# A graph layer and a routed feed-forward layer on one core: sorting nodes by expert during the gather stage, and edge steps of two octets

## The reference

```python
msgs = features[edge_src] * edge_weight[:, None]          # features = layernorm(x)
agg  = segment_sum(msgs, edge_dst, num_segments=12500)
x    = x + einsum('ni,oi->no', agg, W) + b
xf   = layernorm(x)
H    = gelu(xf @ W1 + b1, approximate=False)              # 1024 hidden columns
probs = softmax(H @ Wg + bg)                              # 8 experts
assign = argmax(probs)
out  = x + probs[:, assign] * (H @ Wd[assign] + bd[assign])   # Wd: 8 x 1024 x 256
```

## Time and profile before

| | us |
|---|---|
| median of 3 runs | 3659.71 (3659.63 to 3661.93) |
| the profiled execution | 3686.61 |
| its span, first to last instruction | 3684.6 |
| gather stage (105.38 to 3088.04) | 2982.66 |
| last group, routing, 105 routed tiles | 596.6 |

### The profile page before, as it was taken

One profiled execution on the slowest core, in us unless ns is written; L12 is line 12 of the kernel. 1 busy time (PEld: TensorE's weight loads), 2 busy tenths in 40 slices (PEclk: granted clock), 3 DMA queues, 4 the chain that ended last, 5 costly groups with the idle time before them and its releaser, 6 DMA issues.

```text
span 3684.6 us, 40719 instructions
## 1 busy us (share of the span) xinstructions
PE 2061.4 (56%) x10526; PEld 1319.5 (36%) x10527; DVE 1151.1 (31%) x3507; ACT 443.2 (12%) x847; POOL 1822.5 (49%) x1988
## 2 busy tenths in 40 slices
PE   0134555455535554455445544555355548599998
PEld 0112332233323332233223322332233324488887
DVE  8121332233323332233223322332133224733332
ACT  5000000000000000000000000000000002043343
POOL 1656445644565445544664455444644540055554
PEclk9995666566656666566656656666566658799999
DMA  8323332333333332333233323332333231455554
GB/s 358 88 82 98 97 103 84 115 99 98 104 91 106 100 101 83 113 100 101 84 115 100 102 81 111 98 102 86 105 103 100 82 92 63 154 180 180 181 184 139
DMA packets 153598, 420.31 MB, mean 114 GB/s; under 512 B 33320, under 2 KB 67499, under 8 KB 150880
## 3 DMA queue, kind: packets, MB, share of 16 engines
q0 software_dynamic: 100032, 300.27, 27.6%
q1 hardware_dynamic: 53536, 119.73, 8.8%
HBM read 328.02 MB, written 92.82 MB: 114 GB/s over the span
## 4 chain that ended last, share of the span: by engine, by line
PE 38%; another core or an unknown queue 33%; issue 15%; DVE 7%; DVEq 5%; ACT 1%; DMA 0%; POOL 0%; ACTq 0%; POOLq 0%
PE psH L557 8%; PE psE L507 6%; PE psA L638 3%; PE psG L638 2%; PE psH L638 2%; PE psE L638 2%; PE psA L578 2%; PE psG L499 2%; PE psR L499 2%; PE psA L535 2%; DVEq L301 2%; DVE rows L942 1%; DVEq L295 1%; PE psG L564 1%
## 5 line engine op out<-in xcount | busy, mean ns | idle before, releaser
L387 POOL DMA_INDIRECT big<-xn_table,src_i x1664 | 1590.8, 956 | 1427.4 <-PE psG L499 620.8
L507 PE MATMUL psE<-place,parts 128*128 128x64 f32 x1664 | 450.8, 433 | 1015.3 <-DVE parts L853 778.4
L507 PEld LDWEIGHTS psE<-place,parts 128*128 128x128 f32 x1664 | 382.6, 324 | 1280.6 <-DVE parts L853 871.7
L557 PE MATMUL psH<-xn2T,w 128*128 128x512 f32 x800 | 427.9, 692 | 128.6 <-issue 64.5
L450 ACT ACTIVATE hidT<-psH,b 128x512 f32<-128x512 f32 x200 | 136.4, 687 | 2447.2 <-remote 1006.6
L499 PE MATMUL psR<-big,sel_narrow 128*32 128x256 f32 x1664 | 216.8, 613 | 289.4 <-issue 289.4
L557 PEld LDWEIGHTS psH<-xn2T,w 128*128 128x128 f32 x800 | 173.4, 223 | 347.8 <-issue 267.6
L860 DVE TENSOR_TENSOR big<-psE,big 128x128 f32 x416 | 121.2, 291 | 545.1 <-remote 294.3
L853 DVE COPY parts<-psR 128x256 f32<-128x256 f32 x208 | 88.0, 423 | 518.6 <-remote 461.2
L499 PE MATMUL psG<-big,sel_narrow 128*32 128x256 f32 x1664 | 217.6, 613 | 0.0
L864 DVE TENSOR_TENSOR place<-iota,shift_f 128x256 f32<-128x256 f32 x104 | 44.4, 427 | 447.7 <-issue 447.7
(11 more groups left out here) (194 smaller groups left out, 2193.4 us busy)
## 6 DMA issues: line engine op xcount, KB each, us to landing
row_table<-rows SPq DMA_DIRECT2D x25, 2064.0 KB
big<-xn_table,src_i POOLq DMA_INDIRECT x1664
big<-in_x SPq DMA_DIRECT2D x10, 1280.0 KB, 17.5
xn_table<-big SPq DMA_DIRECT2D x10, 1280.0 KB, 12.9
big<-in_x SPq DMA_DIRECT2D x25, 512.0 KB
row_table<-big SPq DMA_DIRECT2D x25, 512.0 KB, 3.0
big<-in_Wd SPq DMA_DIRECT2D x8, 1024.0 KB, 12.0
hidT<-in_dstT SPq DMA_DIRECT2D x2, 840.0 KB, 30.3
```

The costliest lines, as they stand in the source:

```text
L387: nc.gpsimd.indirect_dma_start(out=xring[:, h * STEP_TILES + j, :], out_offset=None, in_=xn_dram[:, :], in_offset=bass.IndirectOffsetOnAxi ...
L507: mm = nc.tensor.matmul(psE[q % 2][:, k * NARROW:(k + 1) * NARROW], parts[:, q % 2, k * P:(k + 1) * P], place[:, q, :], start=True, stop=True)
L557: mm = nc.tensor.matmul(psH[c % 2][:, :], w1[:, k, c * P:(c + 1) * P], xn2T[:, k, :], start=(k == 0), stop=(k == KC - 1))
```

## The change

**Edge steps.** A section is now two octets of eight tiles. Pairs of tiles share 32 lanes (16 each) and accumulate in PSUM, so 16 partial matmuls (still 256 columns each) fill one `psQ` of 512 columns; DVE copies it once; four place matmuls of 80 columns replace eight of 64; two adds replace four; one table operation each replaces two. `s_edge_mm` rises once, by 16, after all 16 partials, instead of by 4 after each quad. The wide way, for sections whose tiles or octets span too many nodes, stays.

```diff
-                    def partial(q):
-
-                        pe.wait_ge(s_narrow, g * 2 + q // 2 + 1)
-                        for j in range(QUAD):
-                            t = h * STEP_TILES + q * QUAD + j
-                            mm = nc.tensor.matmul(psQ[q % 2][j * LANES:(j + 1) * LANES, 0:C], sel_narrow[:, t, :],
-                                                  xring[:, t, :], start=True, stop=True)
-                        mm.then_inc(s_edge_mm, QUAD)
...
+                    pe.wait_ge(s_narrow, g + 1)
+                    for o in range(OCTS):
+                        for odd in range(2):
+                            for j in range(OCT // 2):
+                                t = h * STEP_TILES + o * OCT + 2 * j + odd
+                                mm = nc.tensor.matmul(psQ[j * LANES:(j + 1) * LANES, o * C:(o + 1) * C],
+                                                      sel_narrow[:, t, :], xring[:, t, :],
+                                                      start=(odd == 0), stop=(odd == 1))
+                    mm.then_inc(s_edge_mm, STEP_TILES)
+
+                    pe.wait_ge(s_parts, g + 1)
+                    for o in range(OCTS):
+                        for k in range(KC):
+                            at = (o * KC + k) * SPAN
+                            mm = nc.tensor.matmul(psE[:, at:at + SPAN], parts[:, o, k * P:(k + 1) * P],
+                                                  place[:, o, :], start=True, stop=True)
+                    mm.then_inc(s_placed, 1)
```

```diff
+            def routed_hidden(r, i):
+
+                pe.wait_ge(s_c2, r + 2)
+                for c in range(HC):
+                    if c % 4 == 0:
+                        pe.wait_ge(s_g2, r * HC + c + 4)
+                    for k in range(KC):
+                        mm = nc.tensor.matmul(psH[c // 4][:, (c % 4) * P:(c % 4 + 1) * P],
+                                              w1[:, k, c * P:(c + 1) * P], xT2[i][:, k * P:(k + 1) * P],
+                                              start=(k == 0), stop=(k == KC - 1))
+                    if c % 4 == 3:
+                        mm.then_inc(s_h2, 1)
+
+            def product(r, i, rounds):
+
+                pe.wait_ge(s_wl[i], rounds * 16 + 16)
+                pe.wait_ge(s_r2, r + 1)
+                for c in range(HC):
+                    pe.wait_ge(s_g2, r * HC + c + 1 + HC)
+                    mm = nc.tensor.matmul(psY[:, 0:C], hT2[:, c, :], wd[:, i, c, :],
+                                          start=(c == 0), stop=(c == HC - 1))
+                mm.then_inc(s_y2, 1)
```

```diff
-                with pe.If(kind == SECTIONS):
-                    before = n.with_bounds(min_val=0, max_val=NF - 2)
-                    hidden(before, before + 1)
-                    transpose_xn2(before + 1)
+                with pe.If(kind == SECTIONS):
+                    part_a(n.with_bounds(min_val=0, max_val=LAST - 1), QB)
+                with pe.If(kind == SECTIONS + 1):
+                    part_b(n.with_bounds(min_val=0, max_val=LAST - 1), QB)
```

More of the change, by code:

```diff
@@ L190, in build @@
[L190 to L196, removed]
@@ L271, in build @@
+        s_i2 = sem("routed_ids_dve")
         s_o2 = sem("routed_out_ready")
[L272 to L295, removed]
@@ L297, in step_field @@
-        def step_field(load, k, a, b, engine, top):
-            return load(steps_i[0:1, bass.ds(k, 1), a:b].rearrange("a b c -> a (b c)"), engine, top)
+        s_os = [sem(f"routed_out_stored{i}") for i in range(RING2)]
+        s_back = [sem(f"routed_out_loaded{h}") for h in range(SECTIONS)]
+        s_out = [sem(f"out_scattered{h}") for h in range(SECTIONS)]
         def load_columns(ap, engine, top):
@@ L303, in load_columns, with step_field, step_count, tiles_of @@
                 skip_runtime_bounds_check_because="columns and kinds are worked out within their bounds")[1]
+        def step_field(k, a, b, engine, top):
+            return load_columns(steps_i[0:1, bass.ds(k, 1), a:b].rearrange("a b c -> a (b c)"), engine, top)
+        def step_count(k, a, eng, engine):
+            raw, = nc.values_load_multi_w_load_instructions(
+                steps_i[0:1, bass.ds(k, 1), a:a + 1].rearrange("a b c -> a (b c)"), engines=(engine,),
+                skip_runtime_bounds_check_because="cut to its low eight bits below")[1]
+            return eng.snap(raw & 255, min_val=0, max_val=255).with_bounds(min_val=0, max_val=NG)
+        def tiles_of(f):
+            return [f * PER_GROUP + i for i in range(PER_GROUP)]
         block = ctx.enter_context(nc.Block())
@@ L368, in _ @@
+            for a in range(0, REST, PER_GROUP):
+                for j, (row, expert) in enumerate(tile_plan(a, min(a + PER_GROUP, REST))):
+                    load_tile(EARLY + a + j, row, expert)
         @block.gpsimd
@@ L381, in _ @@
             pool.wait_ge(s_xn_stored, 16 * LN_CHUNKS)
-            def gather_section(g):
+            for g in range(NG):
                 h = g % SECTIONS
@@ L431, in _ @@
+            for j in range(REST):
+                pool.wait_ge(s_o2, EARLY + j + 1)
+                scatter(late_rows[:, j, :], EARLY + j, s_out[0])
+            totals = [16 * sum(len(batches[b]) for b in range(h, len(batches), SECTIONS)) for h in range(SECTIONS)]
+            totals[0] += 16 * REST
+            for h in range(SECTIONS):
+                pool.wait_ge(s_out[h], totals[h])
         @block.scalar
@@ L447, in hidden @@
[L447 removed]
+                    nc.scalar.activation(xn2T[:, k, 0:nq * P], psH[k][:, 0:nq * P], ACT.Identity).then_inc(s_xtc, 1)
                 for c in range(HC):
                     act.wait_ge(s_h, f * HC + c + 1)
[L450 removed]
+                    nc.scalar.activation(hidT[:, c, 0:nq * P], psH[c % 2][:, 0:nq * P], ACT.Gelu,
                                          bias=b1[:, c:c + 1]).then_inc(s_gelu, 1)
@@ L478, in _ @@
+            copy_routed(EARLY)
+            for r in range(EARLY, NR):
+                gelu_routed(r)
+                if r + 1 < NR:
+                    copy_routed(r + 1)
+                residual(r)
         @block.tensor
@@ L586, in hidden, with gate @@
-                mm.then_inc(s_g, 1)
+                def gate():
+                    pe.wait_ge(s_gc, f + 1)
+                    pe.wait_ge(s_c2, f * PER_GROUP + 2 + 2)
+                    for q in range(nq):
+                        mm = nc.tensor.matmul(psL[:, q, :], gate_parts[:, q * P:(q + 1) * P],
+                                              fold[:, :], start=True, stop=True)
+                    mm.then_inc(s_g, 1)
+                routed_pair(f * PER_GROUP + 2, f * 2 + 1, gate, lambda: pe.wait_ge(s_dif, f + 1))
@@ L655, in _ @@
+            part_a(LAST, LAST_QB)
+            part_b(LAST, LAST_QB)
+            pe.wait_ge(s_ev, LAST * QB + LAST_QB + 1)
+            transposes(EARLY, 0, EARLY // RING2)
+            for r in range(EARLY, NR):
+                routed_hidden(r, r % RING2)
+                if r + 1 < NR:
+                    transposes(r + 1, (r + 1) % RING2, (r + 1) // RING2)
+                product(r, r % RING2, r // RING2)
         @block.vector
@@ L1104 @@
+            for r in range(EARLY, NR):
+                routed_out(r, r % RING2, r - EARLY, r // RING2, True)
 def kernel(**inputs):
```

1130 lines of the change are left out of this document (613 added, 517 removed).

## The result

The changed kernel takes 4275.25 us (median of 4 runs, 4268.27 to 4314.99), the kernel before 3659.67: ratio 1.171, 95% interval 1.165 to 1.177. It is slower by 616 us. The forecast was 4155. The profiled execution is the 4315 one (span 4313.3); the forecast's sum for a profiled execution was 4181, so 132 us are missing from it.

The account below looks back on a forecast made before the run. PE's chain with DVE, its results told late while POOL issues gathers, bounds the gather stage. Start 115, stage 3845 and end 221 make 4181; plus 2, less 27 gives about 4155 us, range 3250 to 4480.

Parts of the forecast that it names:

- the stall: Gather stage: PE's matmuls are told as done late while POOL issues gathers; 979 us before, 9.4 a section.
- The sum at full speed: Whole changed kernel without late PE results: 115 start, 967 gather steps, 1872 groups, 221 end, together 3175 us.
- The stall in the changed kernel: Gather stage after the change: PE's results still come late beside POOL's issuing, 9.7 us a section, stage 3845 us.
- 6.5 us for each part: Parts A and B of each group: each follows a step and loses 6.5 us to late PE results.
- a gather step, table reading and branch about 3.2 us: Gather step: table reading and branch take about 3.2 us of the 9.3 us forecast for the step.
- 48 steps come right after a part and run at 9.3: Gather stage: 48 steps after a part, with POOL's ring full, run at 9.3 us each, 446 us together.
- Both waits are met at once, so POOL issues 20 us without a break: POOL's gathers: both section waits are met after all 16 partials, so 16 gathers at 1.25 us go out unbroken.
- The end: After the last gather step: last group's parts, plan and block copies, 16 late tiles; 221 us instead of 597.
- SP is late: Rival: SP's ordered store, copies and loads delay each part's tiles 10 us, 480 more; chance 0.14 shared with a longer stall.
- Two routed tiles in each part, the hidden layer twice: Groups: two routed tiles a part, 14.2 us, hidden layer computed twice; parts 27 and 51, 1054 us more in all.
- no stall: Rival: the number of hand-overs in edge steps, not POOL's issuing, slows PE; steps run at 9.3, 3150 us; chance 0.14.
- half a stall: Rival: with fewer hand-overs a stalled gather step costs perhaps 3.5 us, giving 3514 us; chance 0.18.

Follow-up runs that it names:

- a_nowide: The changed kernel with the never-taken wide way's code and its branch removed from PE and DVE, gathers as they are: 4295 us.
- a_nowide_nogather: The changed kernel without the wide way's code on PE and DVE, and with only the first 48 gathers issued: 3085 us.
- a_nw_memset: The changed kernel without the wide way's code, each gather after the first 48 replaced by four POOL memsets on an unread tile: 3080 us.
- b_nogather: The kernel before with only the first 48 gathers issued, their rows read again for every section: 2702 us.
- a_nw_pause4: The changed kernel without the wide way's code, POOL waiting after every fourth gather until its gathers land: 3552 us, 0.971 of the kernel before.

## Why the prediction was right, and where it was not

The direction and the size held: 4155 forecast, 4275 measured, inside 3250 to 4480. The way to it did not quite: the changed kernel is braked mostly by something that the forecast did not have, and that the total came out near is luck as far as the reload hides the stall and costs about as much. By its steps:

- **The stall and its 979 us** in the kernel before: right, and the best-borne number. Without gathers the profiled execution takes 2702 us, against the sum of 2706.
- **The sum at full speed**, 3175: with gathers and reload gone it is 3085. The change's own cost in work is 3085 - 2702 = 383 us (forecast 469). The excess stood in the parts and steps, as the table shows.
- **The stall in the changed kernel**: the forecast in fact describes a_nowide (4295 measured in its profiled execution, 4181 forecast), a kernel without the reload. Even there one term was off: 6.5 us for each part, which is itself more than the 5.7 that the earlier trace rows give (6.91 + 5.64, less two hand-overs of 1.71 and messages of 3.4), against 5.8 for part A and 13.9 for part B. Mean times from the first partial, or first matmul of a part, to that of the next step, worked out from PE's rows:

| us | forecast | changed kernel | the same, no gathers | a_nowide | a_nowide, no gathers |
|---|---|---|---|---|---|
| step after part A | 9.3 | 21.4 | 21.8 | 7.7 | 7.7 |
| step after part B | 9.3 | 15.5 | 15.3 | 7.3 | 7.3 |
| step after a step | 21.7 | 18.8 | 18.6 | 22.3 | 9.2 |
| part A | 33.5 | 28.3 | 21.9 | 29.3 | 23.5 |
| part B | 57.5 | 53.0 | 50.5 | 64.4 | 50.5 |

  The step that failed is "a gather step, table reading and branch about 3.2 us" and with it "48 steps come right after a part and run at 9.3": in the changed kernel they take 21.4 and 15.5. It cost 870 us for 47 of them where 446 stood for 48. It was hidden in the total because the stall shrank beside it: steps after a step took 18.8 instead of 21.7, parts 81.3 a pair instead of 91. The steps take the same with and without gathers; what the gathers still cost in the changed kernel is 6.4 us a part A and 2.5 a part B, 214 us in all. The forecast looked at how many instructions a step issues and not at how many stand in DVE's loop, nor at the page's row of instruction packets, which tells of it at once.
- **"Both waits are met at once, so POOL issues 20 us without a break"**: true, but no change. The waits of before were mostly met in time too, and its 1664 gathers went out in 111 unbroken runs for 104 sections (now 101).
- **The end**: 279 instead of 221. The 16 late tiles went faster than the 9 us forecast (one scatter each 7.3 us, 116 in all), but the last group's part A took 65 instead of 20, from PE's first matmul of it to that of part B, and it is as long (69) with gathers and reload gone. The trace of the changed kernel names the wait (first four lines; the other three are the same wait again, between part B and the late tiles):

```profile
4045.57 17.98 SPq L380 DMA_DIRECT2D expert_bins<-sorted_rows  x15
4079.34 0.35 SPq L358 DMA_DIRECT2D xr<-expert_bins  x1
4081.46 0.21 DVE L1053 TENSOR_SCALAR live<-part,limit 128x1 f32<-128x1 f32 x1 [37.10 <-DMA xr<-expert_bins]
4081.53 0.66 PE L612 MATMUL psT<-ident,xr 128*128 128x128 f32 x2 [44.06 <-issue]
...
4134.89 44.20 SPq L380 DMA_DIRECT2D expert_bins<-sorted_rows  x15
4181.20 0.70 SPq L358 DMA_DIRECT2D xr<-expert_bins  x1
4182.70 0.66 PE L612 MATMUL psT<-ident,xr 128*128 128x128 f32 x2 [54.57 <-issue]
```

  PE waits at L609 for the rows of a bin, and SP starts their load only behind the block copies of the group before. This is the rival "SP is late": no edge steps lie between here. It costs 44 us in part A, and 55 of PE's time where the plan and the copies had 22 (at most 35).
- **Two routed tiles in each part, the hidden layer twice**: right in size: part B 50.5 us unhindered (51), part A 23.5 (27).
- **Rivals**: "no stall" and "half a stall" fall with a_nowide and a_nowide_nogather. The first stood on the number of hand-overs; the changed kernel has far fewer in its edge steps and stalls as long. "SP is late" costs little in the parts of a_nowide_nogather (PE stands idle ahead of the tiles' first matmuls for 2 us in a part A, and not at all in a part B), but it makes the end long, as shown. The rival that was missing is the reload; priced alone it would have been 4098.
- The rule of the Trainium skill ("SBUF — State Buffer", "Who interferes with whom") that PE waits for nobody and that DMA does not contend with a compute engine: a_nw_memset agrees for memsets on POOL, b_nogather disagrees for the gathers, by 985 us, as far as PE's results are concerned. Whether a port of SBUF has to do with it, no run shows.

With both brakes eased the changed kernel comes to 3552 us (a_nw_pause4, one run), 3% under the kernel before beside it. But the same kind of wait in the kernel before pays more: 3204 us, 10% under that and 25% under the changed kernel. Nor has the change less work: without gathers 3085 stand against 2702.

## What to carry to other kernels

Where one engine issues long runs of indirect gathers and PE's results come late, break the runs up and let them land; find the burst length by trying, since each pause cost the issuing engine 2 us here. Before adding branches of code to an engine's run-time loop, look at the row of instruction packets on the page and at idle time put down to "issue" ahead of the loop's first operation, and keep code that is never taken out of the loop. Where two brakes sit in one chain, taking one away shows nothing: test all four combinations before calling either innocent.

## What the runs showed of the hardware

- Beside a long unbroken burst of indirect gathers from POOL, results of PE's matmuls can be told as done up to 16 us late, mostly 1 to 6 us after the burst's last gather (from 1033 to 1051 in a_nowide; 42 of 55 copies there). The hidden layer's matmuls, which read nothing gathered, came late too. Bursts of 4.7 us hardly do it, memsets on POOL don't. The burst alone does not decide it: in the changed kernel 70 of 71 waits for place matmuls begun 7 to 21 us into a burst end within 3 us. What else it takes, whether the number of rows, their bytes or their semaphore counts do it, and where in PE's path the result is held, stays open; gathers of shorter rows were not tried.
- DVE's loop, grown by two parts, was loaded anew in packets of 8 KB, over 5 a turn (815 for 152 turns). DVE halted 1.4 to 8.4 us after 334 branches ahead of `place` (1 in a_nowide) and stood idle 11.3 us ahead of each step instead of 2.3 with the short loop; beside gathers or without them alike (1178 and 1184 us in all).
